# Causal attention and mixture of experts on one core: one value tile in two reduced-precision parts, output halves summed by VectorE, last head's low parts on VectorE

## What is computed

```python
qkv = x @ W_qkv.T                      # 16 heads of 32
attn = einsum('bhqd,bhkd->bhqk', q, k) * SCALE
attn = where(causal, attn, -inf)
probs = softmax(attn)
out = einsum('bhqk,bhkd->bhqd', probs, v) ... @ W_proj.T
x = x + layernorm(attention(layernorm(x)))
x = x + layernorm(moe(layernorm(x)))   # 16 experts of 352, top 6
```

## Time and profile before

| what | us |
|---|---|
| three runs | 1725.71, 1728.47, 1731.80 |
| median | 1728.47 |
| span of the profiled execution | 1725.0 |
| PE busy in the span | 1660.5 (96%) |
| DVE busy | 1165.6 (68%) |
| ACT busy | 1105.1 (64%) |
| POOL busy | 949.1 (55%) |

### The profile page before, as it was taken

The page is one execution under the profiler, slowest core; times in us unless marked ns, Lnnn a source line. Parts: engine busy times, 40 slices in busy tenths (PEclk is TensorE's granted clock), DMA queues, the critical chain, the costliest instruction groups (busy, mean ns, idle before and its releaser), DMA issues.

```text
span 1725.0 us, 30537 instructions
## 1 busy us (share of the span) xinstructions
PE 1660.5 (96%) x9262; PEld 1368.8 (79%) x9262; DVE 1165.6 (68%) x2371; ACT 1105.1 (64%) x1684; POOL 949.1 (55%) x834
## 2 busy tenths in 40 slices
PE   7999999999999999999986999999999999999996
PEld 7987667767677777775665899999999999999992
DVE  6437777777777777778697666666665566556554
ACT  3222888778878878877586566665665566556544
POOL 2321888888888888886764343333434333343422
PEclk9999999999999999999997999999999999999998
DMA  8676211111111111112663997897987887788776
GB/s 242 191 219 198 55 50 50 49 49 49 49 49 49 49 49 49 49 49 62 228 238 111 296 276 220 252 268 208 280 240 192 230 260 216 213 247 240 188 194 218
DMA packets 103716, 276.88 MB, mean 161 GB/s; under 512 B 19833, under 2 KB 37625, under 8 KB 93625
## 3 DMA queue, kind: packets, MB, share of 16 engines
q1 hardware_dynamic: 78169, 213.29, 37.8%
q0 software_dynamic: 25440, 62.27, 17.3%
HBM read 194.75 MB, written 63.72 MB: 150 GB/s over the span
## 4 chain that ended last, share of the span: by engine, by line
PE 84%; DVE 6%; DMA 3%; issue 3%; POOL 2%; ACT 2%; SPq 0%; DVEq 0%; ACTq 0%; POOLq 0%
PE p_prj L91 25%; PE a_op L886 11%; PE a_mp L845 8%; PE a_sp L904 7%; PE p_at_ps L91 7%; PE p_logit_ps L91 6%; PE e_qp L91 5%; PE a_op L877 4%; PE p_ht_ps L2060 3%; PE e_vp L91 3%; PE p_at_ps L2083 2%; DVE part_max L763 2%; PE a_sp L908 1%; PE a_shared L863 1%; PE a_mp L848 1%
## 5 line engine op out<-in xcount | busy, mean ns | idle before, releaser
L713 POOL TENSOR_TENSOR prob_lo<-prob,prob_hi 128x1024 fp32r<-128x1024 f32 x217 | 465.6, 2167 | 123.7 <-DVE prob_hi L791 122.4
L763 DVE TENSOR_REDUCE part_max<-a_mp 128x1 f32<-128x512 f32 (+2 forms) x600 | 359.3, 609 | 70.8 <-PE a_mp L845 40.8
L1449 POOL DMA_INDIRECT acc_rows<-m_y_out,m_row_ids x108 | 175.5, 1625 | 412.5 <-ACT m_y_out L1618 387.6
L748 ACT ACTIVATE prob<-a_sp 128x1024 f32<-128x1024 f32 x320 | 293.8, 930 | 66.2 <-PE a_sp L908 36.0
L91 PE MATMUL p_prj<-m_w_hi,m_ht_hi 128*128 128x352 f32 x888 | 297.3, 335 | 1.8 <-DVE m_ht_lo L1858 1.4
L91 PE MATMUL p_prj<-m_w_lo,m_ht_hi 128*128 128x352 f32 x888 | 288.1, 324 | 0.0
L91 PE MATMUL p_prj<-m_w_hi,m_ht_lo 128*128 128x352 f32 x888 | 287.4, 324 | 0.0
L1882 DVE TENSOR_TENSOR m_w_lo<-m_w_raw,m_w_hi 128x704 fp32r<-128x704 f32 (+1 forms) x357 | 270.7, 797 | 23.5 <-ACT m_w_hi L1624 23.1
L1624 ACT ACTIVATE m_w_hi<-m_w_raw 128x704 fp32r<-128x704 f32 (+1 forms) x357 | 229.0, 713 | 19.4 <-PE p_prj L91 16.8
L1868 DVE TENSOR_TENSOR m_at_lo<-p_at_ps,m_at_hi 128x384 fp32r<-128x384 f32 x111 | 61.8, 556 | 253.0 <-ACT m_at_hi L1610 253.0
L735 ACT ACTIVATE prob_hi<-prob 128x1024 fp32r<-128x1024 f32 x216 | 203.2, 941 | 6.9
(11 more groups left out here) (315 smaller groups left out, 3367.5 us busy)
## 6 DMA issues: line engine op xcount, KB each, us to landing
m_w_raw<-wexp SPq DMA_DIRECT2D x51, 1408.0 KB
m_w_raw<-wexp SPq DMA_DIRECT2D x51, 768.0 KB
qk_parts<-rows SPq DMA_DIRECT2D x64, 256.0 KB, 3.2
multi<-qk_parts SPq DMA_DIRECT2D x42, 256.0 KB, 5.0
acc_rows<-p_zeros SPq DMA_DIRECT2D x2, 4352.0 KB, 18.6
v_head<-v_all SPq DMA_DIRECT2D x16, 520.0 KB, 3.0
k_stack<-qk_parts SPq DMA_DIRECT2D x21, 256.0 KB, 4.0
q_stack<-qk_parts SPq DMA_DIRECT2D x21, 256.0 KB, 6.2
```

The source lines that it names most:

```text
L713: nc.gpsimd.tensor_tensor(prob_lo[:, t % RING, :, c0:NB], prob[:, t % RING, :, c0:NB], f32(prob_hi[:, t % RING, :, c0:NB]), ALU.subtract). ...
L748: nc.scalar.activation(prob[:, t % RING, :, c0:NB], sp_[:, t % 2, :, c0:NB], ACT.Exp, scale=SCALE).then_inc(prob_ready, 1)
L763: nc.vector.reduce_max(part_max[:, qb, kb:kb + 1], mp[:, n % 2, 0:width], AX_X).then_inc(piece_done, 1)
L1449: nc.gpsimd.indirect_dma_start(acc_dram[sum_of(t)], bass.IndirectOffsetOnAxis(ap=row_id(t), axis=0), y_out[:, t % 4, :], None, compute_op= ...
```

## The change

It does three things, all in `attention`.

1. In heads 0 to 14 tile 7 leaves `WHOLE`: ACT makes its high part, POOL its low part, PE multiplies both. In the last head tile 7 stays whole.
2. DVE adds the two output halves as it reads a_shared in PSUM (a TENSOR_REDUCE over the pair, in place of the copy); POOL's addition, its semaphore and o_turned go. POOL keeps the product.
3. In the last head DVE makes the low parts of tiles 4, 8, 10, 11, 12 and 16 as well; POOL keeps that of tile 0.

```diff
-WHOLE = {7, 17, 18}
+WHOLE, WHOLE_LAST = {17, 18}, {7, 17, 18}
 HI_DVE, HI_DVE_LAST = {2, 3, 9}, {1, 2, 3, 4, 5, 8, 9, 11, 13, 15, 19}
-LO_POOL, LO_POOL_LAST = set(range(NS)) - {0, 1, 10} - WHOLE, {0, 4, 8, 10, 11, 12, 16}
+LO_POOL, LO_POOL_LAST = set(range(NS)) - {0, 1, 10} - WHOLE, {0}
...
+def whole_tiles(h):
+    return WHOLE_LAST if isinstance(h, int) and h == H - 1 else WHOLE
...
         def store_out(h, g, j):
 
             pool.wait_ge(out_read, g + 1)
-            nc.gpsimd.tensor_tensor(o_sum[:], o_turned[:, :, 0:HD], o_turned[:, :, HD:2 * HD], ALU.add
-                                    ).then_inc(out_summed, 1)
-            pool.wait_ge(out_summed, g + 1)
             pool.wait_ge(recip_done, g + 1)
...
             nc.vector.reciprocal(recip[:], turned[:, :, 2 * HD:VW]).then_inc(recip_done, 1)
-            nc.vector.tensor_copy(o_turned[:], turned[:, :, 0:2 * HD]).then_inc(out_read, 1)
+            nc.vector.tensor_reduce(o_sum[:], turned[:, :, 0:2 * HD].rearrange("p a (s c) -> p a c s", s=2), AX_X, ALU.add
+                                    ).then_inc(out_read, 1)
...
-            if t in lo_pool_tiles(h) | WHOLE:
+            if t in lo_pool_tiles(h) | whole_tiles(h):
                 return
...
-            if t in WHOLE:
+            if t in whole_tiles(h):
```

More of the change, by code:

```diff
@@ L595, in attention @@
     max_rows_b = sb("max_rows_b", [NT - QA, P], F32R)
-    o_turned = sb("o_turned", [P, NTB, 2 * HD], F32)
     recip = sb("recip", [P, NTB, 1], F32)
@@ L616, in attention @@
     max_turned, out_turned, out_stored = sem("a_max_turned"), sem("a_out_turned"), sem("a_out_stored")
-    out_read, out_summed, recip_done = sem("a_out_read"), sem("a_out_summed"), sem("a_recip_done")
+    out_read, recip_done = sem("a_out_read"), sem("a_recip_done")
     def heads(eng, head):
@@ L632, in wait_hi @@
         else:
-            eng.wait_ge(hi_act, h * (NS - len(HI_DVE | WHOLE)) + (t - count_before(tiles | WHOLE, t) + 1))
+            eng.wait_ge(hi_act, h * (NS - len(HI_DVE | WHOLE)) + (t - count_before(tiles | whole_tiles(h), t) + 1))
     def wait_lo(eng, h, t):
@@ L640, in wait_lo @@
         else:
-            eng.wait_ge(lo_dve, h * (NS - len(LO_POOL | WHOLE)) + (t - count_before(tiles | WHOLE, t) + 1))
+            eng.wait_ge(lo_dve, h * (NS - len(LO_POOL | WHOLE)) + (t - count_before(tiles | whole_tiles(h), t) + 1))
     def sync_part(sp):
@@ L731, in high_part @@
         def high_part(h, t):
-            if t not in hi_dve_tiles(h) | WHOLE:
+            if t not in hi_dve_tiles(h) | whole_tiles(h):
                 c0 = S_TILES[t][2]
```

## The result

The changed kernel takes 1734.62 us (median of 6 runs, 1732.42 to 1735.34) against 1726.86 of the kernel before (6 runs on the same chip, 1725.71 to 1731.80): ratio 1.004, interval 1.0029 to 1.0052. It is slower by 0.4%. The profiled execution took 1732.42 us with a span of 1730.7; that of before had a span of 1725.0, so the two traces differ by 5.7 us.

The account below looks back on a forecast made before the run. PE holds 84% of the chain of waits. Loop heads +8.4, head 0 +1.3 and last head -3.15 make +6.55 us, on 1728.5 giving 1735.0 us, 0.4% slower; range 1720 to 1745.

Parts of the forecast that it names:

- Tile 7 on PE: Heads 0 to 14: two fp32 matmuls become four of 0.235 us; PE gains 0.77 us per head if nothing takes it back.
- lo(8) late: Loop heads: POOL's low part of tile 8 ends at 432.22, where it ended at 430.51.
- hi(9): Loop heads: DVE's CAST for tile 9 waits for POOL's low part, ending at 432.77 instead of 431.60.
- lo(10): Loop heads: DVE's low part of tile 10 waits for POOL's of tile 9, ending at 436.30 instead of 435.13.
- PE at E: Loop heads, step 13: PE stalls about 1.3 us for DVE before this piece, making each head 0.6 us longer.
- second rival: Loop heads: the late start is regained, the 0.6 us loss shrinks to nothing; 1726.6 us, chance 0.13.
- Head 0: First head: DVE waits 1.99 us for POOL, against 1.30 in the loop; PE loses 1.3 us, bounds -0.77 and +1.3.
- The sum of the halves: DVE's reduction from PSUM: 0.42 us against the copy's 0.39, ends 0.39 and 0.84; POOL's addition goes; cost 0.
- third rival: Steps 13 to 18: the strided reduction keeps DVE from catching up, all heads lose 1.3 us; 1744.9 us, chance 0.12.
- Last head: PE's 3.15 us of idle time behind POOL's low parts all goes; ends -2.0 and -3.5.
- Waits of POOL for hi(9) shrink to nearly 0: Sign in a loop head: POOL, which waited 1.17 us for DVE's high part of tile 9, hardly waits any more.
- first rival: Loop heads: DVE and POOL do not collide, every head keeps its 0.77 us; 1713.8 us, chance 0.17.

Follow-up runs that it names:

- part 1 alone: Kernel before with only tile 7 split in heads 0 to 14, POOL still summing the halves: 1746.67 us, ratio 1.0116.
- part 2 alone: Kernel before with only DVE's reduction in place of the copy and without POOL's addition: 1726.86 us, ratio 1.0001.
- foreign operation: Changed kernel with tile 7 whole again, plus an unread 1024-element subtraction on POOL in step 7: 1733.47 us, ratio 1.0035 to the kernel before.

## Why the prediction was right

It gave 1735.0 us, and 1734.62 was measured; the sum, +6.55 on the span, came out as +5.7, of which -1.66 lies ahead of the change. Without that the parts make +7.3. The mechanism was right, but the agreement to 0.4 us is luck. The forecast set out from 1728.47, the median of three runs; over six it is 1726.86, 1.6 less, while the medians differ by 7.8 and not by 6.5, and the two misses cancel. Nor is a median 3.47 above the span as a rule: each run of this case took 1.7 to 1.85 us more than its own span, and the rest of the 3.47 was scatter between runs. Step by step:

- **Tile 7 on PE.** -0.77 at C was the step; the trace has -0.81. Right.
- **hi(7) on ACT at nothing.** Right: the idle time of the earlier trace rows covers it.
- **lo(8) late.** Its end was put at 432.22; it is 435.46 - 3.21 = 432.25.
- **hi(9).** Put at 432.77; it is 432.80. The CAST took 1.91 instead of 0.68.
- **lo(10).** Put at 436.30; it is 436.36, and its 2.71 us stand against "about 2.6".
- **PE at E.** The stall was put at about 1.3, with L763 as its releaser; it is 1.24. PE goes on with 0.33 from E to the next matmul, as in the earlier trace rows, so E counts as 437.12 on before's time, against 437.05 in the prediction and 436.42 before. The difference of 0.70 is what a head has grown by, 0.69. The prediction had 0.6 (0.63 by its own 437.05, rounded down), hence 1.25 of the 14 heads' 9.65 us were missing.
- **Nothing is regained behind E.** Right: the shift at E is the head's. The second rival, 1726.6, falls by that.
- **Head 0.** +1.3 was the step. The two stalls are there, 0.38 and 1.15 us, and from the wait for v_head to the first turn it is +1.36. Two other differences lie in that stretch. In the trace after, PE's granted clock is 0.51 and 0.54 (the level of 1.2 GHz) from 170.80 to 174.40, after a wait for the load of v_head, and full behind it; before, it is 1.00 there. And the stall of 1.28 us in the earlier trace rows is missing after. The trace of part 1 alone separates them: there the clock is full in this stretch, the first stall is there (1.26), and so are the two others (0.46 and 1.13). From head 0's first scores to the first turn it has 33.81, against 33.86 in the changed kernel and 32.51 before. So +1.3 is borne out, and the two differences balance.
- **The sum of the halves.** 0.42 was taken, 0.39 is measured: 64 times, 391 to 395 ns, where the copy took 385 to 395. The lower bound is the value, and 128 results cost no more than one. The third rival, that this reduction keeps DVE from catching up, falls, and part 2 alone shows it (ratio 1.0001).

```profile
L785 DVE TENSOR_REDUCE o_sum<-a_shared x64: 391/394/395, 184.4 to 825.7; 128x128 f32<-128x256 f32 x64
```

- **Last head.** -3.15 was the term, with -3.5 if the short waits around went too; -3.68 is measured. PE's idle time in that stretch fell from 3.22 to 0.47 us: the three waits went, and the 0.40 behind ACT's o_sb came, the engine named as next in line. The other 0.93 is in PE's recorded busy time, 44.80 instead of 45.73 us for 228 matmuls in both, which the trace does not divide further. Without part 1 the median is 1723.08 against 1727.01 for the kernel before on the same chip, -3.9, and the loop's heads are unchanged there.
- **What was wrong.** "Waits of POOL for hi(9) shrink to nearly 0": the one before lo(9) went from 1.17 only to 0.63, since POOL waits from its own end until the CAST is through, 0.55, and 0.08 more. In the total over the heads nothing shrank (84.3 and 85.4 us), because POOL's wait for hi(2) of the next head grew from 4.33 to 4.89. This hung on no term of the sum. The prediction should have seen it: its own walk put lo(9) at 432.85, 0.63 behind lo(8)'s 432.22.

The first rival, with its 1713.8, supposed that there was no collision. The foreign operation settles it: an unread subtraction on POOL makes a CAST on DVE 1.14 us longer and the head 0.68 longer. The Trainium skill's rule (SBUF — State Buffer, "Who interferes with whom") agrees in who blocks whom: copies and subtractions between SBUF on one engine with those on the other, reductions out of PSUM with neither. How long the blocked one needs after the other's end, 0.55 and 1.08 us, is this case's number.

## What to carry to other kernels

When work moves onto POOL, look at every SBUF-to-SBUF instruction of DVE that falls into its new time, not at whether POOL has idle time: here an engine busy for 54% made a head 0.7 us longer, by an instruction on another engine that shares no data with it. Put the added work where that other engine reads PSUM or waits: the same split on tile 17 instead of tile 7 turned +0.4% into -0.6%. And a saving on the bounding engine is kept only as far as the next wait on another engine, so read what is due just behind the place, the transfers too.

## What the runs showed that was not expected

Which of the two engines goes first when POOL has its next instruction ready is not fixed. In the version with tiles 17 and 18 split, heads 1 to 14, DVE's lo(18) is recorded from 0.42 to 0.52 us before the end of POOL's low part, and POOL's product is next. In 4 of the 14 heads DVE goes first and takes 1.50 or 1.55 us; in 10 POOL's product and lo(19) go first as well, and it takes 3.15 to 3.21. POOL in a head where DVE went first, then DVE in the head before it and in that one:

```profile
491.31 1.38 POOL L704 TENSOR_TENSOR rows<-o_sum,recip 128x128 f32 x1
```

```profile
450.55 3.15 DVE L799 TENSOR_TENSOR prob_lo<-prob,prob_hi 128x1024 fp32r<-128x1024 f32 x1
...
490.93 1.50 DVE L799 TENSOR_TENSOR prob_lo<-prob,prob_hi 128x1024 fp32r<-128x1024 f32 x1
```

At 490.93 the product is the one that waits (1.38 us instead of 0.40). The Trainium skill has it that the order of issue decides who blocks (SBUF — State Buffer, "Who interferes with whom"); the trace does not bear that out here by its recorded starts, since DVE's lies ahead of the product's in all 14. What decides between the two was not found. DVE's start lay 0.42 to 0.47 us before the end of POOL's low part where it went first, and 0.45 to 0.52 where it did not. From one turn of lo(18) to the next the head is 40.2 to 40.3 us after DVE went first, and about 40.4 otherwise.

One thing goes with it in all eleven traces. Where POOL had waited before the low part that holds DVE off, DVE's low part went ahead of POOL's next instruction every time: at lo(10) in the 15 heads of ten kernels, the kernel before and the changed one among them. Where POOL had come straight from its instruction before, POOL went first in 26 of 30 cases: in all 15 heads of the changed kernel with hi(9) on ACT, where DVE's lo(10) was recorded 0.73 us or more ahead of POOL's end, and in 11 of the 15 lo(18). That is a pattern in the rows and no cause; no run tried it. It is why the walk of the prediction was safe: hi(9) of DVE stands between POOL's lo(8) and lo(9), so POOL always waits there. The prediction took it for granted that DVE's lo(10) goes before the product, and there it did not hold.
